# Sums of keys times values: two full-precision matmuls replaced by six of rounded parts and remainders

## The reference

```python
Q = heads(proj(query, Wq, bq))
K = heads(proj(query, Wk, bk))
V = heads(proj(query, Wv, bv))
phiQ = elu_plus_one(Q)
phiK = elu_plus_one(K)
S = jnp.einsum('bhki,bhkj->bhij', phiK, V)
Z = phiK.sum(axis=-2)
num = jnp.einsum('bhqi,bhij->bhqj', phiQ, S)
denom = jnp.einsum('bhqi,bhi->bhq', phiQ, Z)[..., None] + EPS
```

## Time and profile before

| | |
|---|---|
| median of 3 runs | 983.43 us |
| the profiled execution | 983.66 us |
| its span, first to last instruction | 981.8 us |
| TensorE busy | 964.2 us |
| VectorE busy | 502.9 us |
| ScalarE busy | 291.3 us |
| granted TensorE clock | full (2.4 GHz) in all slices |

### The profile page before, as it was taken

One profiled execution on the slowest core, in us unless ns is written; L12 is line 12 of the kernel. 1 busy time (PEld: TensorE's weight loads), 2 busy tenths in 40 slices (PEclk: granted clock), 3 DMA queues, 4 the chain that ended last, 5 costly groups with the idle time before them and its releaser, 6 DMA issues.

```text
span 981.8 us, 13335 instructions
## 1 busy us (share of the span) xinstructions
PE 964.2 (98%) x4865; PEld 816.0 (83%) x4865; DVE 502.9 (51%) x1034; ACT 291.3 (30%) x557; POOL 114.3 (12%) x168
## 2 busy tenths in 40 slices
PE   5999999999999999999999999999999999999998
PEld 4887888877889998978786888777788999999986
DVE  6886577768543465662313455547557113122354
ACT  6873132232133243421223122114223212145300
POOL 7101001001020010000000000000302003074100
PEclk9999999999999999999999999999999999999999
DMA  7413013113020033224302555525523202010054
GB/s 259 166 49 88 4 43 105 42 28 107 29 65 23 22 129 113 92 102 166 109 1 64 185 183 174 194 86 188 167 86 108 86 1 86 1 44 1 23 192 140
DMA packets 57113, 92.03 MB, mean 94 GB/s; under 512 B 23996, under 2 KB 34540, under 8 KB 57024
## 3 DMA queue, kind: packets, MB, share of 16 engines
q1 hardware_dynamic: 48544, 62.47, 19.4%
q0 software_dynamic: 8480, 28.45, 8.9%
HBM read 66.72 MB, written 24.17 MB: 93 GB/s over the span
## 4 chain that ended last, share of the span: by engine, by line
PE 60%; DVE 2%; ACT 0%; issue 0%; DMA 0%; DVEq 0%; ACTq 0%
PE PS L1644 7%; PE PS L1643 7%; PE PS L1645 7%; PE PS L1702 5%; PE PS L1704 4%; PE PS L1523 4%; PE PS L1522 4%; PE PS L1524 4%; PE PS L1723 3%; PE PS L1722 3%; PE PS L1721 3%; PE PS L1774 2%; PE PS L1775 2%; PE PS L1773 2%; PE PS L1504 1%; PE PS L1685 1%
## 5 line engine op out<-in xcount | busy, mean ns | idle before, releaser
L1522 PE MATMUL PS<-ring,act_t 128*128 128x512 f32 (+1 forms) x480 | 193.5, 403 | 1.5 <-DVE act_t L1052 1.5
L1524 PE MATMUL PS<-ring,act_t 128*128 128x512 f32 (+1 forms) x480 | 190.4, 397 | 0.0
L1523 PE MATMUL PS<-ring,act_t 128*128 128x512 f32 (+1 forms) x480 | 190.2, 396 | 0.0
L1643 PE MATMUL PS<-act_t,ring 128*128 128x416 f32 (+1 forms) x432 | 152.4, 353 | 0.0
L1644 PE MATMUL PS<-act_t,ring 128*128 128x416 f32 (+1 forms) x432 | 152.2, 352 | 0.0
L1645 PE MATMUL PS<-act_t,ring 128*128 128x416 f32 (+1 forms) x432 | 151.8, 351 | 0.0
L1522 PEld LDWEIGHTS PS<-ring,act_t 128*128 128x128 f32 (+1 forms) x480 | 89.7, 187 | 23.6 <-DVE act_t L1052 2.3
L1524 PEld LDWEIGHTS PS<-ring,act_t 128*128 128x128 f32 (+1 forms) x480 | 89.4, 186 | 22.3
L1523 PEld LDWEIGHTS PS<-ring,act_t 128*128 128x128 f32 (+1 forms) x480 | 89.7, 187 | 20.4
L1643 PEld LDWEIGHTS PS<-act_t,ring 128*128 128x128 f32 x432 | 81.3, 188 | 3.1
L1644 PEld LDWEIGHTS PS<-act_t,ring 128*128 128x128 f32 x432 | 81.4, 188 | 0.7
(11 more groups left out here) (197 smaller groups left out, 1659.5 us busy)
## 6 DMA issues: line engine op xcount, KB each, us to landing
stage_x<-in_wslices_dram POOLq DMA_DIRECT2D x54, 256.0 KB, 3.9
stage<-in_wslices_dram POOLq DMA_DIRECT2D x42, 256.0 KB, 3.1
xr<-x_d SPq DMA_DIRECT2D x18, 512.0 KB, 3.7
xrow<-in_x_dram SPq DMA_DIRECT2D x9, 512.0 KB, 3.7
xh<-in_x_dram SPq DMA_DIRECT2D x18, 256.0 KB
x_d<-xh SPq DMA_DIRECT2D x18, 256.0 KB
x_d<-xr SPq DMA_DIRECT2D x9, 512.0 KB, 3.1
out_dram<-xr SPq DMA_DIRECT2D x9, 512.0 KB, 2.6
```

Source lines behind the costliest of these rows:

```text
L1522: pe.matmul(out_ap, node_rows(0, k, t), ring[:, slot(k0 + k), 0, :], start=(k == 0), stop=False)
L1523: pe.matmul(out_ap, node_rows(1, k, t), ring[:, slot(k0 + k), 0, :], start=False, stop=False)
L1524: ins = pe.matmul(out_ap, node_rows(0, k, t), ring[:, slot(k0 + k), 1, :], start=False, stop=(k == KD - 1))
L1643: pe.matmul(out_ap, w[0], x_t[:, 0, k, o:o + n], start=(k == 0), stop=False)
```

## The change

The two matmuls of `kv_sum` become six: `vt` and `phik` are each split in a rounded part and a remainder, and hi x hi, hi x lo and lo x hi are added up. ScalarE writes `vt` directly in rounded form and makes the rounded part of `phik` (`phik_h`). VectorE makes both remainders, `vt_l` (from PSUM) and `phik_l`, and gives the PSUM bank back with the first of them. The exponential is made in place in `kmin`, and `phik` in `kb`; both have one buffer instead of two, and the first `kb` operation of a step waits for the `phik_l` of the step before.

```diff
--- before.py
+++ after.py
@@ -230,11 +230,12 @@
             keys = sb("keys", [P, ROWL + EXTRA_CHUNKS, 2], F32, r2)
             kcur = sb("kcur", [P, 2, 2, KEY_SLOTS], I16, r2)
             cadd = sb("cadd", [P, 8, P], U16, r2)
-            kb = sb("kb", [P, 2, 256], F32, r2)
-            vt = sb("vt", [P, 2, 256], F32, r2)
-            kmin = sb("kmin", [P, 2, 256], F32, r2)
-            kexp = sb("kexp", [P, 2, 256], F32, r2)
-            phik = sb("phik", [P, 2, 256], F32, r2)
+            kb = sb("kb", [P, 256], F32, r2)
+            vt = sb("vt", [P, 2, 256], F32R, r2)
+            kmin = sb("kmin", [P, 256], F32, r2)
+            vt_l = sb("vt_l", [P, 2, 256], F32R, r2)
+            phik_h = sb("phik_h", [P, 2, 256], F32R, r2)
+            phik_l = sb("phik_l", [P, 2, 256], F32R, r2)
             ksum = sb("ksum", [P, D], F32, r2)
             iota_c = sb("iota_c", [P, P], F16, r2)
             ident_u = sb("ident_u", [P, P], U16, r2)
@@ -330,6 +331,10 @@
         kmin_ready = sem("kmin_ready")
         kexp_ready = sem("kexp_ready")
         phik_ready = sem("phik_ready")
+        vt_hi = sem("vt_hi")
+        vt_lo = sem("vt_lo")
+        phik_hi = sem("phik_hi")
+        phik_lo = sem("phik_lo")
         ksum_ready = sem("ksum_ready")
         s_done = sem("s_done")
         st_ready = sem("st_ready")
@@ -832,12 +837,13 @@
                 for w in counted[:2]:
                     adj_out(w)
                 act.wait_ge(kmin_ready, step + 1)
-                nc.scalar.activation(kexp[0:r, step % 2, :], kmin[0:r, step % 2, :], ACT.Exp).then_inc(kexp_ready, 1)
+                nc.scalar.activation(kmin[0:r, :], kmin[0:r, :], ACT.Exp).then_inc(kexp_ready, 1)
                 u = UNIT["kv", step // NT, step % NT]
                 if step >= 2:
                     act.wait_ge(s_done, sums_of(step - 2))
-                nc.scalar.activation(vt[0:r, step % 2, :], PS[0:r, bank(u), 256:512],
-                                     ACT.Copy).then_inc(acc_free[bank(u)], 1)
+                nc.scalar.activation(vt[0:r, step % 2, :], PS[0:r, bank(u), 256:512], ACT.Copy).then_inc(vt_hi, 1)
+                act.wait_ge(phik_ready, step + 1)
+                nc.scalar.activation(phik_h[0:r, step % 2, :], kb[0:r, :], ACT.Copy).then_inc(phik_hi, 1)
                 if step < 7:
                     ln_root(step + 3)
                 for w in counted[2:]:
@@ -1206,8 +1212,10 @@
                 u = UNIT["kv", s, t]
                 wait_full(dve, u)
                 dve.wait_ge(kvb_in[s % 2], 16 * (s // 2 + 1))
-                link(dve.tensor_tensor(kb[0:r, b, :], PS[0:r, bank(u), 0:256], kvb[0:r, s % 2, 0:256], ALU.add))
-                dve.tensor_scalar(kmin[0:r, b, :], kb[0:r, b, :], 0.0, None, ALU.min).then_inc(kmin_ready, 1)
+                if step:
+                    dve.wait_ge(phik_lo, step)
+                link(dve.tensor_tensor(kb[0:r, :], PS[0:r, bank(u), 0:256], kvb[0:r, s % 2, 0:256], ALU.add))
+                dve.tensor_scalar(kmin[0:r, :], kb[0:r, :], 0.0, None, ALU.min).then_inc(kmin_ready, 1)
                 if step < 7:
                     dve.wait_ge(x_in[(step + 3) % 2], 16 * ((step + 3) // 2 + 1))
                     ln_stats(step + 3)
@@ -1219,14 +1227,19 @@
                 dve.wait_ge(kexp_ready, step + 1)
                 if step >= 2:
                     dve.wait_ge(s_done, sums_of(step - 2))
-                dve.scalar_tensor_tensor(phik[0:r, b, :], kb[0:r, b, :], 0.0, kexp[0:r, b, :],
+                dve.scalar_tensor_tensor(kb[0:r, :], kb[0:r, :], 0.0, kmin[0:r, :],
                                          ALU.max, ALU.add).then_inc(phik_ready, 1)
                 dve.wait_ge(phik_ready, step + 1)
                 z = ksum[0:r, 256 * s:256 * s + 256]
                 if t == 0:
-                    dve.tensor_copy(z, phik[0:r, b, :]).then_inc(ksum_ready, 1)
+                    dve.tensor_copy(z, kb[0:r, :]).then_inc(ksum_ready, 1)
                 else:
-                    dve.tensor_tensor(z, z, phik[0:r, b, :], ALU.add).then_inc(ksum_ready, 1)
+                    dve.tensor_tensor(z, z, kb[0:r, :], ALU.add).then_inc(ksum_ready, 1)
+                dve.wait_ge(vt_hi, step + 1)
+                dve.tensor_tensor(vt_l[0:r, b, :], PS[0:r, bank(u), 256:512], vt[0:r, b, :].bitcast(F32),
+                                  ALU.subtract).then_inc(acc_free[bank(u)], 1)
+                dve.wait_ge(phik_hi, step + 1)
+                dve.tensor_tensor(phik_l[0:r, b, :], kb[0:r, :], phik_h[0:r, b, :].bitcast(F32), ALU.subtract).then_inc(phik_lo, 1)
                 if step < 7:
                     dve.wait_ge(ksum_ready, step + 1)
                     ln_finish(step + 3)
@@ -1530,13 +1543,16 @@
 
                 s, t = divmod(step, NT)
                 r = rows(t)
-                pe.wait_ge(phik_ready, step + 1)
+                pe.wait_ge(phik_lo, step + 1)
                 wait_read(pe, UNIT["kv", s, t])
                 for p in range(2):
                     o = 256 * (s % 2) + P * p
-                    ins = pe.matmul(PS[:, 3 + s // 2, o:o + P], vt[0:r, step % 2, P * p:P * (p + 1)],
-                                    phik[0:r, step % 2, P * p:P * (p + 1)], start=(t == 0 and p == 0),
-                                    stop=False, skip_group_check=True)
+                    q = slice(P * p, P * (p + 1))
+                    v = [vt[0:r, step % 2, q], vt_l[0:r, step % 2, q]]
+                    k = [phik_h[0:r, step % 2, q], phik_l[0:r, step % 2, q]]
+                    for i, j in ((0, 0), (0, 1), (1, 0)):
+                        ins = pe.matmul(PS[:, 3 + s // 2, o:o + P], v[i], k[j], start=(t == 0 and p + i + j == 0),
+                                        stop=False, skip_group_check=True)
                 ins.then_inc(s_done, 1)
                 if t == NT - 1:
                     pe.wait_ge(ksum_ready, step + 1)
```

## The result

The changed kernel took 997.32 us (median of 4 runs, 996.64 to 999.22), the kernel before 983.42 us (983.35 to 983.93). The ratio is 1.0144, with a 95% interval of 1.0132 to 1.0156: 13.9 us slower, where 13.0 were predicted. The scatter is wider than before: two executions (996.64, 996.69 us) have a mean granted clock of 1.000, the two longer ones (997.95, 999.22 us) 0.998. The profile is of the longest, 15.6 us over the span of before, so it shows about 2.5 us that the shortest runs don't have.

What follows compares the result with a forecast made beforehand. TensorE was taken as the bound, busy 964.2 of 981.8 us. Six products 7.8, first steps 3.7 and step 30 1.5 sum to 13.0 us, so 983.4 + 13.0 = 996.4 us; range 987 to 1004.

Steps and rivals of the forecast that it cites:

- TensorE's term: In the 40 kv_sums, six products limited by their loads take 0.65 instead of 0.44 us: +7.8 us in all.
- The shading of window steps to +0.16: In 23 steps followed by bf16 products, only five of six products grow: about +0.16 us instead of +0.21.
- fast loads: Rival: rounded 128-column loads go fast, 60 ns a product; TensorE gains 3.2 us; chance 0.09.
- four passes: Rival: a short rounded product takes all four passes in kv_sum, +35 us, total about 1017; chance 0.05.
- The first steps: Until step 6, layer norm of later tiles shares VectorE's and ScalarE's queues, so TensorE waits: together +3.7 us.
- step 3: Worked example of the early steps: phik_h delays ScalarE's root, so ln_finish starts 1.55 us later, against 1.33 us of slack.
- The edge rows in step 4: VectorE work that stood in idle time, 1.26 us, comes onto the path.
- The loop's 7.27 us: Early VectorE and ScalarE round, kb to kb, against TensorE's 7.1: 0.17 us lost in each of five steps, 0.85 us.
- the edge order of step 6: VectorE work formerly in idle time, put at about 1 us, comes onto the path.
- Step 30: VectorE's added work makes one-hot tiles later, so TensorE waits +1.5 us more; ends 0 and 2.3.
- falls elsewhere in the new program: Lower end, 0, of the step-30 wait: VectorE's 2.94 us idle is a code fetch behind a skipped branch and moves.
- only TensorE's term: Rival: VectorE's and ScalarE's additions stay hidden, leaving 983.4 + 7.8 = 991.2 us; chance 0.22.

Runs made afterwards that it cites:

- two_full_both: Changed kernel with layer norm ahead of the split work in steps 0 to 6, no all_counts branch, two full-precision matmuls instead of six products: 984.57 us.
- six_only: Kernel before with six products of the same rounded tiles in place of two matmuls, nothing added on VectorE and ScalarE: 990.67 us.
- stat64: Changed kernel with 64 instead of 128 stationary columns in the six products of tiles 1 to 9 (36 of 40 steps): 994.74 us.
- no_branch: Changed kernel without the branch around all_counts, a path never taken with these inputs, on VectorE and TensorE: 993.99 us.
- two_full: Changed kernel with two full-precision matmuls of the rounded parts instead of six products; remainders made but not multiplied: 994.97 us.
- pool_late: Changed kernel, but GpSimd splits weight slices 8 and 9 only after the second kv_sum: 998.99 us.
- ln_first_no_branch: Changed kernel with layer norm's root ahead of phik_h and ln_finish ahead of the remainders in steps 0 to 6, and no all_counts branch: 991.81 us.
- stream64: Changed kernel with 64 instead of 128 streamed columns in each of the six products: 998.66 us.

## Why the prediction was right, and where it was not

The 13.9 us split by the differences of four times: 983.4 before; the work on VectorE and ScalarE with both remedies 1.2 (two_full_both); six products 7.2; the order of the early steps and the branch 5.5. Such differences add up to 997.3 whatever the cause; that each step is what its name says is shown by the traces. The branch stood in the kernel before too, at 0.5 us there.

**TensorE's term: right, by its mechanism.** +7.8 predicted; 7.9 in the trace, 7.0 and 7.2 by six_only and two_full_both, in which some waits shrink as TensorE comes later. The choice to price a product by its load (107 ns with one streamed column) held: 0.11 us with 128 stationary columns, 0.06 with 64. The shading of window steps to +0.16 was wrong: they grow by 0.19 to 0.20, as the others do on average. The lower bound taken from the bf16 one-hot products is what bf16 operands really give, 0.35 us for six; rounded float32 does not load that way. The rivals of fast loads and of four passes are out. The Trainium skill, "TensorE: Matmul & The Clock Gate", section "Back-to-back issue gap", would have made the term an estimated 2 us; the 0.11 us between products speaks against it for this type, while the bf16 products are even closer (0.055 us) than its 81 ns.

**The first steps: size right (3.7 against 3.2 of waits), half of the path wrong.** In step 3 itself the working holds. VectorE's first and last word there:

```profile
45.88 0.41 DVE L1217 TENSOR_TENSOR kb<-PS,kvb 128x256 f32<-128x256 f32 x1
...
50.80 0.17 DVE L1046 RECIPROCAL ln<-ln 128x1 f32<-128x1 f32 x1 [0.93 <-issue]
```

From `kb` to `ln_finish` it has 4.92 us instead of the 3.36 of the earlier trace rows, 1.56 later, where 1.55 was predicted. The edge rows in step 4 were foreseen at 1.26 us, and the wait that they cause, at the start of TensorE's step 6, is 1.16. The loop's 7.27 us was near the 7.19 of this trace and of stat64, but this is hardly longer than TensorE's own 7.10, so the 0.85 us over five steps did not appear (in no_branch, with rounds of 7.18, some 0.1 us for each). Nor did the wait for the edge order of step 6 (0.18 instead of about 1) and that of step 8. The edge order is there, 68.69 to 69.74 on VectorE; but TensorE has as much more to do in step 6, also before the change (its `kv_sum`s start at 55.05 and 62.90, 7.85 us apart instead of 6.9), which the prediction left out. In their place came step 2, where GpSimd holds two VectorE operations. The step that failed is "Take step 3", as a pattern for the others: how long VectorE's operations last depends on GpSimd in the first 30 us, and step 3 has no GpSimd beside it. That the lower clock would follow and take another 1.6 us was no term of the sum. And 0.4 of the 3.2 us is the wait at 19.52, ahead of the first `kv_sum`, which the traces of two_full and pool_late have too and the rest don't.

**Step 30: right in sum, wrong in place.** +1.5 predicted, 1.8 measured, but at the tiles of step 30 the waits grew from 0.8 to only 1.25 us. The other 1.32 us is at those of step 20. The end "falls elsewhere in the new program" was half of the truth: one idle stayed near step 30 with 2.17 us instead of 2.94, and a second one of 2.14 came up ahead of the tile at 169.80.

The total came within 0.9 us in part because such errors cancelled. The rival "only TensorE's term" (991.2) describes ln_first_no_branch, but not the kernel as changed.

## What to carry to other kernels

- Price a short matmul by its loads and their type. Here a full-precision matmul of 128 columns had two (4 for a `kv_sum`, 0.44 us) and three single-pass ones have three (6, 0.63 us): more loads, at 0.11 us each.
- Removing work from the bounding engine gives back only what the next engine's queue allows: two_full returned 2.4 us of 7.2 until VectorE's hiccups were gone. Look for idle marked as issue and for operations longer than their like before you price a speed-up.
- A pause of 1.2 to 1.7 us can cost twice: once as a wait, once in the clock behind it.

## What the runs showed of the hardware

- VectorE operations on 128x256 with a usual 0.29 to 0.42 us took 0.90 to 1.63 us beside a GpSimd operation; which one is caught changes from kernel to kernel.
- Behind waits of 1.18 (stream64), 1.47, 1.49, 1.57 (stream64) and 1.73 us TensorE ran up to 3.5 us at 1.2 GHz (matmuls of 512 columns 0.43 us apart instead of 0.23); behind the 1.16 us at 61.74, the 1.32 at 175.65 and the 1.64 in two_full it did not. So the length of the wait alone doesn't decide it; what does stays open.
- A branch that jumps over unused code left VectorE idle for 2.1 to 2.9 us at one to three of ten places, and for 0.4 to 1.5 us at four or five more; which ones changed with the program around it.
